# Transformer block with 32 routed experts: the low halves of expert weights made in two steps of the tile loop

## The reference, cut to what matters

```python
x = x + tanh(g_xattn) * softmax(layernorm(scores(layernorm(x), ctx)))     # 4 x 512 x 512
h = layernorm(x)                                                        # 2048 tokens of 512
scores = sigmoid(h @ gate_w)                                            # 32 experts
topk_idx = top 4 experts of a token, out of its 2 best groups of 8
topk_w = scores[topk_idx] / (sum + 1e-20) * 2.5
up = einsum('th,ehi->tei', h, Wu); act = relu(up) ** 2                    # Wu: 32 x 512 x 256
routed = einsum('tei,te,eih->th', act, combine, Wd)                     # Wd: 32 x 256 x 512
out = x + tanh(g_ffn) * (routed + relu(h @ Wsu) ** 2 @ Wsd)
```

## Time and profile before

| what | us |
|---|---|
| median of 3 runs | 582.55 (581.95 to 583.17) |
| the profiled execution, its own time | 585.93 |
| its span, first to last instruction | 584.1 |
| PE, DVE, ACT, POOL busy | 553.8, 407.4, 334.3, 193.8 |
| expert loop, first to last up product of tiles 3 to 80 | about 283 |
| granted TensorE clock, mean | 0.989 of full speed |

### The profile page before, as it was taken

How to read it: one execution, slowest core, us unless ns; L and a number is a source line. 1 busy time by engine, 2 the same in 40 slices (tenths; PEclk the granted TensorE clock), 3 DMA queues, 4 the chain that set the end, 5 groups by cost and what they waited for, 6 DMA issues and landing times.

```text
span 584.1 us, 10807 instructions
## 1 busy us (share of the span) xinstructions
PE 553.8 (95%) x3021; PEld 438.9 (75%) x3022; DVE 407.4 (70%) x887; ACT 334.3 (57%) x658; POOL 193.8 (33%) x197
## 2 busy tenths in 40 slices
PE   6988999998999999999999999999889999999993
PEld 4456876776688878898888988889879898864441
DVE  5698894583878947565767667675765656717997
ACT  4668673745327844666666667666756776731210
POOL 3110000000000042556666565665545656430000
PEclk9998999999999999999999999999998999999997
DMA  8920101006000025967787786778777686679997
GB/s 307 360 99 0 68 6 72 2 1 217 1 1 0 2 83 183 378 224 251 260 285 247 251 291 224 250 265 273 216 271 276 221 291 220 208 245 361 390 399 275
DMA packets 60769, 116.40 MB, mean 199 GB/s; under 512 B 5909, under 2 KB 24470, under 8 KB 60694
## 3 DMA queue, kind: packets, MB, share of 16 engines
q1 hardware_dynamic: 47728, 73.03, 36.8%
q0 software_dynamic: 12960, 42.48, 20.5%
q10 hardware_dynamic: 6, 0.00, 0.0%
HBM read 85.87 MB, written 29.62 MB: 198 GB/s over the span
## 4 chain that ended last, share of the span: by engine, by line
PE 69%; DVE 16%; issue 5%; DMA 5%; ACT 3%; DVEq 1%; POOL 1%; ACTq 1%; SPq 1%; POOLq 0%
PE U L1499 31%; PE D L1499 26%; DVE X L1485 8%; PE T L1836 5%; PE D L1852 3%; PE T L1499 2%; DMA xg<-h_rows,idx_g 2%; DMA h_rows<-HR 1%; DVE xgT_lo L1358 1%; DVE wd_lo L1353 1%; DMA yg<-y_rows 1%; PE T L1642 1%; DVE HR L942 1%; ACT wu_hi L757 1%; DVE wu_lo L1348 1%
## 5 line engine op out<-in xcount | busy, mean ns | idle before, releaser
L472 POOL DMA_INDIRECT y_rows<-yb,idx_s x81 | 92.0, 1136 | 103.2 <-ACT yb L783 59.4
L465 POOL DMA_INDIRECT xg<-h_rows,idx_g x81 | 87.3, 1078 | 107.9 <-DVE tab L1327 78.7
L783 ACT ACTIVATE yb<-D 128x512 f32<-128x512 f32 x81 | 48.4, 598 | 67.4 <-PE D L1499 50.2
L1358 DVE TENSOR_TENSOR xgT_lo<-T,xgT_hi 128x512 fp32r<-128x512 f32 x81 | 55.6, 686 | 36.7 <-ACT xgT_hi L766 35.1
L1499 PE MATMUL U<-wu_hi,xgT_hi 128*128 x324 | 60.1, 307 | 6.8 <-DVE xgT_lo L1358 3.3
L1499 PE MATMUL D<-wd_hi,eaT_hi 128*128 x162 | 57.9, 438 | 0.0
L1363 DVE SCALAR_TENSOR_TENSOR eact<-U,erel 128x256 f32<-128x256 f32 x81 | 34.0, 420 | 33.6 <-ACT erel L771 22.2
L1485 DVE SCALAR_TENSOR_TENSOR X<-yg,w,X 128x512 f32<-128x512 f32 x64 | 46.8, 750 | 14.1 <-DMA yg<-y_rows 11.4
L1348 DVE TENSOR_TENSOR wu_lo<-wu,wu_hi x32 | 39.2, 1225 | 23.8 <-issue 23.8
L1499 PEld LDWEIGHTS U<-wu_hi,xgT_hi 128*128 128x128 f32 x324 | 45.2, 189 | 12.0 <-issue 11.0
L1499 PE MATMUL U<-wu_lo,xgT_hi 128*128 x324 | 52.6, 284 | 0.0
(11 more groups left out here) (247 smaller groups left out, 1118.2 us busy)
## 6 DMA issues: line engine op xcount, KB each, us to landing
wu<-in_L_ffn_Wu SPq DMA_DIRECT2D x32, 512.0 KB
wd<-in_L_ffn_Wd SPq DMA_DIRECT2D x32, 512.0 KB
yg<-y_rows SPq DMA_DIRECT2D x64, 256.0 KB, 8.5
X<-in_x SPq DMA_DIRECT2D x4, 1024.0 KB, 10.6
h_rows<-HR SPq DMA_DIRECT2D x4, 1024.0 KB, 4.3
out<-X SPq DMA_DIRECT2D x16, 256.0 KB, 8.9
wsu<-in_L_ffn_Wsu SPq DMA_DIRECT2D x2, 1024.0 KB, 7.7
wsd<-in_L_ffn_Wsd SPq DMA_DIRECT2D x2, 1024.0 KB, 8.8
```

What stands on the lines that cost most here:

```text
L465: pool.indirect_dma_start(out=xg[:, u, :], out_offset=None, in_=h_dram[:, :], in_offset=bass.IndirectOffsetOnAxis(ap=idx_g[:, t:t + 1], ax ...
L472: pool.indirect_dma_start(out=y_dram[:, :], in_=yb[:, u, :], in_offset=None, out_offset=bass.IndirectOffsetOnAxis(ap=idx_s[:, t:t + 1], ax ...
L783: ac.activation(yb[:, t % UNROLL, :], D[2 + t % 2][:, :], ACT.Copy)\
L1358: ve.tensor_tensor(xgT_lo[:, t % 2, :, :], T[t % 2][:, :].rearrange("p (h n) -> p h n", h=HB), xgT_hi[:, t % 2, :, :].bitcast(f32), ALU.su ...
```

## The change

On DVE the table entry of tile t+3 is read first in the step, the score portion comes behind `xgT_lo`, and the two weight halves are separated: `wu_lo` stays at the end of step t, `wd_lo` goes to the end of step t+1. The five operations of `weights()` go one each into steps 50 to 54. On ACT the order of the operations is unchanged; the two conditional pieces are put into one branch, whose two sides both hold the step's own operations.

```diff
 # ACT
             def step(t):
-                v = split_of("act", t + 3) if t + 3 < N_TILES else None
+                def own():
+                    tile_relu(t + 1)
+                    tile_actT(t)
+                    if t:
+                        tile_out(t - 1)
+                if t + 3 == N_TILES:
+                    tile_in(t + 2)
+                    own()
+                    return
+                v = split_of("act", t + 3)
                 tile_in(t + 2)
-                if v is not None:
-                    with ac.If(v > 0):
-                        split_up(v)
-                tile_relu(t + 1)
-                tile_actT(t)
-                if t:
-                    tile_out(t - 1)
-                if v is not None:
-                    with ac.If(v > 0):
-                        split_down(v)
+                with ac.If(v > 0):
+                    split_up(v)
+                    own()
+                    split_down(v)
+                with ac.Else():
+                    own()
 # DVE
+            begins = {}
             def step(t):
+                if t + 3 < N_TILES:
+                    begins[t + 3] = split_of("dve", t + 3)
                 tile_in(t + 2)
+                score(t)
                 tile_square(t + 1)
                 tile_actT(t)
+                if t + 2 in begins:
+                    with ve.If(begins[t + 2] > 0):
+                        split_down(begins[t + 2])
                 if t + 3 < N_TILES:
-                    split(t + 3)
+                    with ve.If(begins[t + 3] > 0):
+                        split_up(begins[t + 3])
...
+            def score(t):
+                c = t // 8 - 2
+                if 0 <= c < 4:
+                    if t % 8 == 0:
+                        places_met(c)
+                    elif t % 8 == 3:
+                        scores_met(c)
+                    elif t % 8 == 6:
+                        scores_of(c)
+                elif 50 <= t < 55:
+                    weights(t - 50)
...
             for t in range(NT * TOPK - 2):
                 step(t)
-                c = t // 8 - 2
-                if 0 <= c < 4:
...
-                elif t == 50:
-                    weights()
```

More of the change, by code:

```diff
@@ L1418, in scores_of, with weights @@
                 nth()
-            def weights():
+            w3 = w4[:, :].rearrange("p (t k) -> p t k", k=TOPK)
+            def weights(part):
                 ve.wait_ge(s["dve_ch"], chain[0])
[L1422 to L1434, removed]
+                if part == 0:
+                    i_ = ve.tensor_reduce(wsum[:, :], w3, AX.X, ALU.add)
+                elif part == 1:
+                    i_ = ve.tensor_scalar(wsum[:, :], wsum[:, :], 1e-20, None, ALU.add)
+                elif part == 2:
+                    i_ = ve.reciprocal(wsum[:, :], wsum[:, :])
+                elif part == 3:
+                    i_ = ve.tensor_tensor(w3, w3, wsum[:, :].unsqueeze(2).broadcast_to([P, NT, TOPK]), ALU.mult)
+                else:
+                    i_ = ve.tensor_scalar(w4[:, :], w4[:, :], SCALE, g_tanh[:, 1:2], ALU.mult, ALU.mult)
+                i_.then_inc(s["dve_ch"], 1)
+                nth()
+            def score(t):
[9 more added lines that the diff above has]
+                    weights(t - 50)
             used = load_used(ve)
```

## The result

| kernel | us, median (lowest to highest) | ratio to before |
|---|---|---|
| before, same call | 582.86 (581.95 to 583.55) | |
| changed | 574.03 (572.15 to 575.26) | 0.985 [0.982, 0.988] |

Faster by 8.8 us, where 9.8 were predicted. The profiled execution took 572.15 us, 1.9 under the median, with a span of 570.3; that of before was 3.4 over its median. So the two profiles differ by 13.8 us, and only part of that is the change.

What follows compares the result with a forecast made beforehand. PE was taken as the bound, losing time where DVE's weight splits made xgT_lo late. -12.0 for the splits plus 2.2 for late loads gave -9.8, from the median of 582.55 to 572.7 us; range 567 to 579.

Steps and rivals of the forecast that it cites:

- Where PE's time went: Expert loop, tiles 3 to 80: 16.0 us lost, 12.0 of them to DVE's splits making xgT_lo late for PE.
- The predicted marks: Signs of being right: halves one step apart, xgT_lo early, first tiles 3.5 us, 77 tiles in 271 to 276 us.
- All 29 losses can go: -12.0: DVE's weight splits in the loop: with the halves apart, all 29 losses vanish, -12.0 us; bounds -12.0 and 0.
- each on average: The 12.0 us spread over the loop's 29 DVE splits, 0.41 us for each.
- The table entry is read first ... 0: DVE's step: the read of 0.30 us moves ahead of xgT_lo, off the path once the halves are apart; 0 us.
- Score portions: DVE's portions move ahead of eact with 2.4 us of slack against 1.04; weights()'s 1.3 us delay at tile 53 goes.
- ACT's branch: ACT's step: same operations and order, one branch less where an expert begins, 0.8 us of slack at xgT_hi; 0 us.
- The rival on ACT's code: ACT's longer code and jumps cause stalls of 3.7 us: one more gives 576.4 us, two 580.1; chance 0.10.
- the prediction's own sign of being wrong: New idle time of ACT put down to "remote", listed among the marks that would show the prediction wrong.
- +2.2: Later wd_lo frees the raw slot later, delaying SP's loads; PE stops 2.2 us around tiles 57 to 61; bounds 0 and 13.2.
- 1.3 + 0.87 + 0.87: Weight loads around tiles 57 to 61: 1.3 us late, then two two-tile experts fall back 0.87 each, to 3.0 late.
- The 3.7 us at tiles 59 and 60: Loss there put to another cause, ACT's 2.11 us idle at "remote"; perhaps rare, so left alone on both sides.

Runs made afterwards that it cites:

- call 3: Later call on a chip of its own: halves alone, changed kernel, POOL's order, 40 POOL waits; before 584.79 us, changed again 579.44 us (0.990).
- second profile: Trace of the changed kernel run again without an edit, beside variants on one chip: 579.44 us, 0.990 of before.
- call 1: Kernel before with one part of the change at a time: halves 585.05 us, scores 580.99, table read 582.13, ACT's branch 582.97; before 584.63.
- call 2: Halves plus ACT's branch on the kernel before 577.37 us; changed kernel with late read 577.51, old ACT 574.92, halves together 575.31; before 582.82.
- the other order: Changed kernel with POOL's scatter one tile later, so a gather is issued ahead of the scatter waiting for yb: 575.96 us, 0.984 of before.

## Why the prediction was right, and where it wasn't

**Total.** 572.7 predicted, 574.03 measured, inside the range and the forecast's own 570 to 575. Two of its steps were wrong and hid each other, so that the sum came right is in part luck. It also holds for the call of the result alone: in call 3 the gain was 5.4 us, where 9.8 were predicted.

**Where PE's time went: right.** PE waited for `xgT_lo` at the first tile of each expert. The 16.0 us lost in the loop went to 3.9, and the changed tile shows the 0.8 us of slack that I had worked out (0.87 to 0.89). The predicted marks hold: first tiles of 3.5 us, 77 tiles in 271.1 us, `wu_lo` and `wd_lo` one step apart.

**"All 29 losses can go: -12.0", put to the halves: the wrong owner.** The losses went, but undoing the halves cost about 1 us by ratios from two calls, with intervals that allow none and some 3. The halves would have been enough too (with ACT's branch they gained 5.4); they were not needed. The 0.41 us "each on average" also hid two kinds of tile: 1.1 us at the five with a portion in front, 0.16 at the 23 ordinary ones, and 0.5 of the 12.0 was a gather at tile 6. This step failed because the next one did.

**"The table entry is read first ... 0": wrong.** I took 0.30 us, the median duration of all reads, and asked what it is worth once the halves are apart. I should have asked what it is worth by itself, and looked at the reads of the splits, which took 0.60 on average. The read holds up all that follows it: the branch and, in the trace behind the branch, some 0.5 us of register work for the addresses of the operands, which with the late read comes in part after `eaT_lo`. The idle time ahead of `wu_lo` went from 0.76 to 0.12 us a split, and `wd_lo` gave 0.45 of that back, which leaves about 0.2, near the 0.16 that an ordinary first tile lost. Two parts of the change treat the same loss, each is sufficient at the ordinary splits, and the sum of the two is that of one.

**Score portions: right in size.** The five tiles with a portion ahead of a split lost 5.5 us, part of my 12.0, and moving the portions alone brought 3.6.

**ACT's branch: 0 predicted.** Alone it brought 1.7 us, undone 0.9 by times from two calls, less than the interval. The rival on ACT's code did not come in the result: the changed kernel has no idle time of ACT at "remote" in its first profile, and the profile's page counts 45 packets of fetched code in q14 for 42 before. In its second profile that idle time, the prediction's own sign of being wrong, is there (7.2 us). I had counted engine operations, nine for six, and left out the register work: in the traces ACT carries out 1233 instructions for 1374 before, 131 compare-and-branches for 179, since the second branch of each step fell away. By the Trainium skill (Runtime: NRT & Kernel Launch, Instruction fetch mechanics) a taken branch whose target is outside the fetched window has to wait for its code. No run here shows whether ACT's longer branch leaves that window. The late starts for which I had called on the rule occur with ACT's old and new step alike, and with the same kernel in one call and not in another.

**"+2.2" for the later release: found, but not its size.** ACT waits for weights five times for 3.3 us and once more for 0.6, at tiles 29, 47, 57, 59, 61 and 79, the six places named. PE lost nothing from it in the changed kernel, since none of the waits (1.1 at most) was much over ACT's slack of 0.8. With ACT's or the table's part undone the waits are 7.0 and 6.9 us, and tiles 59 and 61 in the one and tile 57 in the other lose 0.4 to 0.7 each behind `xgT_lo`. The term was there with 0 to 1 us; 2.2 assumed that each tile falls back further, and 1.3 + 0.87 + 0.87 did not add up, since the loads there were issued 7.33 and 7.65 us apart for 7.81.

**The 3.7 us at tiles 59 and 60: right to leave alone, for another reason.** 1.6 are left in the first profile of the changed kernel and 1.2 in the second. There tile 59's part is PE waiting for gather 60, which POOL's stop of 3.1 us ahead of scatter 53 delays; the stop is in the profile of before too, and ACT has no part in it. What was rare in the profile of before is the 1.6 us of tile 60 at half clock, about half of the 3.4 by which that execution was over the median. Its 2.11 us of ACT at "remote" ended as PE got its gather, at 435.71; which of the two held tile 59 there, no run separates.

**Open.** What makes ACT begin up to 2 or 3 us after a product's end on two of the chips; whether the halves alone gain on a chip without that (with ACT's branch they gained 5.4); why the table reads at first tiles are slow; what ACT's one branch saves; and the 2.6 to 3.5 us that the late read still costs beside the halves apart.

## What to carry to other kernels

A value that decides a branch can cost more than the median time of its load: look at the loads where the branch is taken, and at the idle time "issue" ahead of the first instruction behind the branch, and read the value early in the step, while the engine waits anyway. Then see what the instruction behind that one waits for; here it gave back two thirds. When several edits treat one loss, the right total proves none of them; take them out one by one from the full version, since edits made alone can be drowned by something else (here the late starts). And where two calls can land on different chips, run the kernel itself again beside its variants: the same changed kernel stood at 574.0 and at 579.4.

## What the runs showed of the hardware

- ACT began up to 2.2 us (3.1 in call 1) after PE's last product for it had ended by the profile, in calls 1 and 3, each on a chip of its own: 24 times of 0.5 us or more in the loop of one kernel, 1 to 17 in the other seven. On the chip of call 2 no profile has more than one (0.6 us). The changed kernel took 5.4 us more in call 3 than at first; the kernel before took 584.8 there and 582.8 in call 2.
- In both orders tried POOL stopped ahead of its 114th indirect transfer of the loop: 3.68 and 3.70 us of idle time in the rows above, about 3.1 of them over the ordinary start behind `yb`, and 2.08 for 0.30 in the other order.
- A branch on a value just read cost DVE 0.76 us of idle time a split. The reads took 0.60 us on average at the splits and 0.31 in the median of all.
- After idle times of 0.84 and 0.80 us the clock granted to PE fell to 0.5 for 3.4 us in the profile of before, and tile 60 lost 1.6 us.
